# The opening of a four-layer fp32 kernel rebuilt around batch 0's chain, with idle transposes on TensorE

## Time and profile before

| | us |
|---|---|
| runs | 458.79, 456.85, 453.72 (median 456.85) |
| the profiled execution | 456.1, span 454.4, mean granted clock 0.966 |
| PE busy, PE weight loads busy | 395.8 (87%), 370.1 (81%) |
| DVE, ACT, POOL busy | 308.2 (68%), 226.6 (50%), 182.2 (40%) |
| PE in the chain that ended last | 50%; DVE 24%, ACT 12%, POOL 6% |
| `normalise(b, 0)` of the four batches starts at | 80.08, 175.77, 269.97, 364.14 |

### The profile page before, as it was taken

How to read it: one execution, slowest core, us unless ns; L and a number is a source line. 1 busy time by engine, 2 the same in 40 slices (tenths; PEclk the granted TensorE clock), 3 DMA queues, 4 the chain that set the end, 5 groups by cost and what they waited for, 6 DMA issues and landing times.

```text
span 454.4 us, 8501 instructions
## 1 busy us (share of the span) xinstructions
PE 395.8 (87%) x3034; PEld 370.1 (81%) x3034; DVE 308.2 (68%) x929; ACT 226.6 (50%) x622; POOL 182.2 (40%) x300
## 2 busy tenths in 40 slices
PE   0668747699998999999989999999899989998596
PEld 0546636599987998899979997999789979996495
DVE  3479767796786666878765758878665666765343
ACT  0285564456564344656644345656543456564132
POOL 2235283734553433455434334545533332322031
PEclk9988986899999999999999999999999999999699
DMA  7997001000000001100000002000000000000000
GB/s 212 364 343 282 1 0 50 1 2 1 1 0 3 0 1 30 45 1 1 2 1 1 1 1 72 2 1 2 1 1 2 1 23 1 2 2 0 0 1 23
DMA packets 15080, 16.85 MB, mean 37 GB/s; under 512 B 1536, under 2 KB 14016, under 8 KB 15040
## 3 DMA queue, kind: packets, MB, share of 16 engines
q1 hardware_dynamic: 15040, 16.33, 11.1%
HBM read 15.28 MB, written 1.05 MB: 36 GB/s over the span
## 4 chain that ended last, share of the span: by engine, by line
PE 50%; DVE 24%; ACT 12%; POOL 6%; issue 5%; DMA 2%; SPq 1%; DVEq 0%; POOLq 0%; ACTq 0%
PE bank_s L300 13%; PE bank_u L300 10%; PE bank_qa L300 6%; ACT prob L741 6%; DVE prob L1326 5%; PE bank_o L300 4%; PE bank_pt L300 4%; PE bank_pt L471 3%; DVE pt_lo L1337 3%; DVE xn L1140 2%; POOL prob L1000 2%; DVE ut_lo L1343 2%; DMA wq_raw<-in_wqT 2%; ACT ut_hi L707 2%; PE bank_s L568 2%
## 5 line engine op out<-in xcount | busy, mean ns | idle before, releaser
L1000 POOL TENSOR_SCALAR prob<-prob,row_inv,valid_b 128x256 f32<-128x256 f32 x128 | 71.5, 567 | 84.2 <-DVE row_inv L1333 83.6
L741 ACT ACTIVATE prob<-prob,row_min 128x256 f32<-128x256 f32 x128 | 64.1, 502 | 71.5 <-DVE row_min L1326 71.5
L1337 DVE TENSOR_TENSOR pt_lo<-bank_pt,pt_hi 128x512 fp32r<-128x512 f32 x64 | 44.2, 690 | 14.1 <-ACT pt_hi L707 13.8
L1343 DVE TENSOR_TENSOR ut_lo<-bank_u,ut_hi 128x256 fp32r<-128x256 f32 x64 | 27.0, 422 | 38.6 <-ACT ut_hi L707 38.2
L1326 DVE CUSTOM_DVE_ANT_0 prob<-bank_s,masked 128x256 f32<-128x256 f32 x128 | 48.9, 419 | 2.9 <-PE bank_s L300 2.3
L300 PE MATMUL bank_u<-pt_hi,cx_hi 128*128 128x256 f32 x128 | 37.8, 295 | 7.0 <-DVE pt_lo L1337 6.7
L1012 POOL TENSOR_TENSOR act_lo<-act_raw,act_hi 128x256 fp32r<-128x256 f32 x32 | 24.0, 749 | 48.0 <-ACT act_hi L800 48.0
L300 PE MATMUL bank_o<-c_hi,ut_hi 128*128 128x256 f32 x128 | 39.2, 306 | 4.5 <-DVE ut_lo L1343 4.5
L707 ACT ACTIVATE pt_hi<-bank_pt 128x512 fp32r<-128x512 f32 x64 | 37.5, 586 | 10.8 <-PE bank_pt L471 10.8
L471 PE MATMUL bank_pt<-ident,prob 128*128 128x128 f32 x256 | 39.4, 277 | 3.9 <-POOL prob L1000 3.6
L300 PE MATMUL bank_qa<-xt_hi,a_hi 128*128 128x256 f32 x128 | 41.0, 320 | 0.8 <-DVE qa_lo L1315 0.7
(11 more groups left out here) (234 smaller groups left out, 1300.7 us busy)
## 6 DMA issues: line engine op xcount, KB each, us to landing
wq_raw<-in_wqT SPq DMA_DIRECT2D x4, 512.0 KB, 8.8
wo_raw<-in_wo SPq DMA_DIRECT2D x4, 512.0 KB, 9.7
w_raw<-in_w12T SPq DMA_DIRECT2D x1, 1408.0 KB, 9.1
gate_raw<-in_gateT SPq DMA_DIRECT2D x2, 576.0 KB, 8.8
up_raw<-in_upT SPq DMA_DIRECT2D x2, 576.0 KB, 10.5
down_raw<-in_downT SPq DMA_DIRECT2D x2, 576.0 KB, 12.4
x<-in_x SPq DMA_DIRECT2D x4, 256.0 KB, 5.3
guT<-in_guT SPq DMA_DIRECT2D x4, 256.0 KB, 6.8
```

The source lines that it names most:

```text
L741: last = act.activation(row, row, ACT.Exp, scale=-1.0, bias=row_min[:, h % 2, t:t + 1], accum_out=row_sum[:, h % 2, t:t + 1])
L1000: last = pool.tensor_scalar(row, row, row_inv[:, h % 2, t:t + 1], valid_b[:, 0:1], ALU.mult, ALU.mult)
L1337: dve.tensor_tensor(pt_lo[:, :, :].rearrange("p s t -> p (s t)"), bank["pt"][:, :], f32(pt_hi[:, :, :].rearrange("p s t -> p (s t)")), ALU ...
L1343: dve.tensor_tensor(ut_lo[:, :], bank["u"][:, 0:T], f32(ut_hi[:, :]), ALU.subtract).then_inc(S["u_l"], 1)
```

## The change

- **Loads**: the ternary weights (w12 1408 KB, w3 704 KB) move ahead of Wk, Wq, Wv and Wo; the turned expert weights of one batch at a time are loaded, into one buffer, and the mask after.
- **Opening**: PE turns x of batch 0 only (and of batch 1 at its end); x of batches 2 and 3 is normalised, turned and measured in the FFN stage of the batch before the one ahead (`lnq_apply`, `q_weight_scales`, `q_first_scales` at c = 4, 6, 7; `q_turn_xn` on PE at c = 7). POOL's roots and first diagonals for them go between `ffn_low` and `normalise(b+1, 0)`.
- **TensorE**: 94 transposes of the unit matrix into the unused bank `pt`, in four calls of `keep_busy`.
- **Ternary weights** become (w > g) - (w < -g) with g = half the mean magnitude: POOL writes w < -g, DVE takes it from w > g; no ACT pass after. Layer 2's residual is scaled by 0.5 instead of w3.
- **Layer 1**: DVE writes batch 0's diagonals (128x128 each) instead of POOL; gate*up and silu go from POOL to DVE.
- **Prep banks**: 16 units use 6 banks instead of 2.
- **FFN weights**: 12 units of 128x576, all lo parts on POOL: 4 in the opening, 8 inside the heads of batch 0.

```diff
+        PREP_BANKS = ("qa", "o", "s0", "s1", "qa", "o", "s0", "s1", "qa", "o", "qa", "o", "x1", "pt", "o", "x1")
+FFN_LO_HEADS = (1, 2, 5, 6, 7, 8, 13, 14)
# SP
             turned_expert_weights(0)
             expert_weights(0)
+            ternary_weights()
             attention_weights(0)
+            mask(0)
# PE
+            def keep_busy(n):
+                for _ in range(n):
+                    pe.transpose(bank["pt"][:, 0:P], ident[:, :], ident[:, :])
             pe.wait_ge(S["consts"], 2)
-            q_turn_x0()
+            keep_busy(22)
+            q_turn_xn(0)
+            keep_busy(24)
+            q_piece(0, 0)
+            keep_busy(24)
             prep_unit(0)
-            q_piece(0, 0)
+            pe.wait_ge(S["abs_done"], 6)
+            pe.matmul(bank["u"][:, 0:6], ones[:, :], gsum[:, :], ...).then_inc(S["gamma_mm"], 1)
+            q_piece(1, 0)
             prep_unit(1)
+            q_piece(2, 0)
...
+            q_piece(5, 0)
+            q_piece(6, 0)
             prep_unit(7)
+            keep_busy(24)
+            bit_turn(0)
             prep_unit(8)
+            pe.wait_ge(S["limits"], 1)
+            pe.wait_ge(S["w12_ready"], 4)
+            pe.wait_ge(S["prep_lo"], 8)
# ACT
+            act.activation(warm[:, :], ones[:, 0:2], ACT.Exp)
+            act.wait_ge(S["w12_in"], 16)
+            for j in range(2):
+                for k in range(ND):
+                    magnitudes12(j, k)
+            act.wait_ge(S["w3_in"], 32)
+            magnitudes(...)  # w3, two parts
             prep_hi(0)
+            q_bf(0, 0)
# POOL
             q_round(0, 0, 0)
             q_scale_diagonals(0, 0)
+            pool.wait_ge(S["limits"], 1)
+            for j in range(2):
+                for k in range(ND):
+                    ternary12_minus(j, k)
+            q_root1(0)
+            ternary3_minus(0)
+            ternary3_minus(1)
             q_round(0, 1, 0)
             q_scale_diagonals(0, 1)
+            lnq_power(1, 2)
             power(0, "lnb")
+            pool.wait_ge(S["lnb_xn"], 1)
+            ffn_weights_lo(0)
             for c in range(BIT_CHUNKS):
                 bit_low(0, c)
             power(0, "lna")
+            pool.wait_ge(S["lna_xn"], 1)
+            ffn_weights_lo(1)
+            ffn_weights_lo(2)
+            ffn_weights_lo(3)
             normalise(0, 0)
+            q_roots(1)
+            q_spread_diagonals(1, 0)
# POOL, a head of a batch
                     if h == 13:
                         power(b + 1, "lnb")
+                    if b == 0 and h in FFN_LO_HEADS:
+                        ffn_weights_lo(FFN_LO_EARLY + FFN_LO_HEADS.index(h))
# POOL, the end of a batch
                 for c in range(FFN_CHUNKS - 1):
                     ffn_low(b, c)
+                if b + 2 < NB:
+                    q_roots(b + 2)
+                    q_spread_diagonals(b + 2, 0)
                 if not last:
                     normalise(b + 1, 0)
# DVE
             q_ctx_amax(0)
+            q_spread_diagonals0(0)
             q_scaled_w(0, 0)
...
             q_round_w0(0)
+            ternary_limits()
+            q_bf_w(0)
+            prep_lo(0)
             prep_lo(1)
             q_dequant(0, 0)
+            q_half_product(0)
+            q_silu(0)
+            ternary12(0, 0)
             q_ratio1(0)
+            ternary12(0, 1)
+            q_spread_diagonals0(1)
             prep_lo(2)
             q_scaled_w(0, 1)
...
             q_round_w0(1)
+            ternary12(1, 0)
             prep_lo(3)
+            lnq_stats_of([1]); lnq_variances([1])
             q_dequant(0, 1)
             q_residual0()
             ln_stats_of(0, "lnb")
             prep_lo(4)
             ln_apply(0, "lnb")
             prep_lo(5)
+            ternary12(1, 1)
             prep_lo(6)
             ln_lo(0, "lnb", xt_hi, xt_lo)
+            prep_lo(7)
+            ternary3(0)
+            ternary3(1)
# DVE, batch 0's head 9
+                    elif h == 9 and b == 0:
+                        link(lnq_stats_of([2, 3]))
+                        lnq_variances([2, 3])
```

More of the change, by code:

```diff
@@ L207, in build @@
                 S[f"{n}{i}"] = sem(f"{n}{i}_in")
-        for i in range(FFN_UNITS):
+        for i in range(FFN_LOADS):
             S[f"ffn_w{i}"] = sem(f"ffn_w{i}_in")
@@ L690, in _ @@
             queries(0, 1)
+            q_turn_xn(1)
+            prep_unit(14)
             pe.wait_ge(S["ctx_hi"], 1)
@@ L874, in _ @@
-            last.then_inc(S["next_xn"], 1)
-            prep_hi(6)
-            prep_hi(7)
+            for k in range(4, 7):
+                prep_hi(k)
             q_bf(0, 1)
             q_wscale(0, 1)
+            prep_hi(7)
+            for u in range(3):
+                ffn_weights_hi(u)
+            ln_hi(0, "lnb", xt_hi)
             prep_hi(8)
-            act.wait_ge(S["bit_q12"], 1)
-            for j in range(2):
-                act.activation(w12[:, :, j * BIT:(j + 1) * BIT], w12_raw[:, :, j * BIT:(j + 1) * BIT], ACT.Copy,
-                               bias=-MAGIC).then_inc(S["w12_ready"], 1)
-                if j == 0:
-                    prep_hi(9)
@@ L1442, in before @@
                 def before(h):
[L1443 to L1448 removed]
+                    if not last and h == 7:
+                        q_silu(nxt)
                 attention(b, before, beside)
@@ L1487, in batch @@
                             mask_row(nxt)
+                            if b + 2 < NB:
+                                lnq_apply(b + 2)
+                        if c == 6 and b + 2 < NB:
+                            q_weight_scales(b + 2)
                         if c == 5:
@@ L1530, in ternary @@
-            def ternary(part):
-                if part == 0:
-                    for j in range(2):
-                        w = w12_raw[:, :, j * BIT:(j + 1) * BIT]
-                        last = dve.tensor_scalar(w, w, gam[:, j:j + 1], MAGIC, ALU.mult, ALU.add)
-                    link(last)
-                else:
-                    dve.tensor_scalar(w12_raw[:, :, :], w12_raw[:, :, :], MAGIC + 1.0, MAGIC - 1.0, ALU.min, ALU.max
-                                      ).then_inc(S["bit_q12"], 1)
+                link(dve.tensor_scalar(gam[:, :], bank["u"][:, 0:6], 1.0 / (BIT * D), None, ALU.mult))
@@ new lines, in ternary_limits, with ternary12 @@
+                pairs = gam[:, :].rearrange("p (j k) -> p j k", k=2)
+                link(dve.tensor_tensor(above[:, :], pairs[:, :, 0], pairs[:, :, 1], ALU.add))
+                link(dve.tensor_scalar(above[:, :], above[:, :], BIT_EPS, 0.5, ALU.add, ALU.mult))
+                dve.tensor_scalar(below[:, :], above[:, :], -1.0, None, ALU.mult).then_inc(S["limits"], 1)
+            def ternary12(j, k):
+                dve.wait_ge(S["minus12"], 2 * j + k + 1)
+                cols = slice(j * BIT, (j + 1) * BIT)
+                dve.scalar_tensor_tensor(out=w12[:, k, cols], in0=w12_raw[:, k, cols], scalar=above[:, j:j + 1],
+                                         in1=f32(w12[:, k, cols]), op0=ALU.is_gt, op1=ALU.subtract
+                                         ).then_inc(S["w12_ready"], 1)
@@ new lines, in ternary3 @@
+            def ternary3(part):
+                dve.wait_ge(S["minus3"], part + 1)
+                rows, cols = ((P, slice(0, BIT_FULL)), (BIT_REST, slice(BIT_FULL, BIT_CHUNKS)))[part]
+                flat = [t[0:rows, cols, :].rearrange("p c d -> p (c d)") for t in (w3, w3_raw)]
+                dve.scalar_tensor_tensor(out=flat[0], in0=flat[1], scalar=above[0:rows, 2:3], in1=f32(flat[0]),
+                                         op0=ALU.is_gt, op1=ALU.subtract).then_inc(S["w3_ready"], 1)
```

495 lines of the change are left out of this document (224 added, 271 removed).

## The result

The changed kernel takes 459.26 us, the median of 20 runs (456.48 to 461.91); the kernel before takes 455.97 in 20 runs beside them. The ratio is 1.0082, with a 95% interval of 1.0063 to 1.01. The forecast of 447.0 and its range of 440 to 454 both miss. The profiled execution took 460.1, its span is 458.4 at a mean clock of 0.957; with 454.4 before, 4.0 us of span are to be explained, and 13.1 against the 445.3 forecast.

A forecast was written before the change was run, and what follows sets the result against it. It took the opening, up to about 80 us, as bound by a chain of hand-offs PE mostly waits for, later PE work. 454.4 − 11.5 + 2.4 gave 445.3 of span, plus 1.7: 447.0 us, range 440 to 454.

The forecast's parts named there:

- First scaling: First scaling on DVE in the opening: starts at 12.1 us instead of 17.10, 5.0 earlier.
- keep_busy: Four calls of added transposes on PE in the opening: they raise the clock and cost nothing.
- The rival by which transposes don't raise it: PE in the opening: transposes don't hold the clock; 7.7 us more, 454.7; chance 0.12.
- First rounded transposes: PE in the opening, waiting for Wq, taken as in at 17: 18.5 us instead of 21.45, 2.9 earlier.
- Second scaling: DVE in the opening, with POOL's 128x704 pieces at 1.2 us each: 31.2 instead of 33.96, 2.8 earlier.
- One wait of that step: DVE's gate*up, with two SBUF inputs, waits for POOL's last 128x704 piece: done at 24.6 us.
- Residual add: Residual add on DVE in the opening: at 37.4 us instead of 42.54, 5.1 earlier.
- layer 2's add: Layer 2's add on DVE, behind the ternary products: at 56.5 us, 4.9 earlier.
- Normalise of layer 2: DVE's normalise, for which POOL now waits: 0.73 us instead of 5.31, a further 4.6 earlier.
- From there on: From head 0's `pt_lo` to the end, heads and FFN stages: added work and savings sum to 2.4 us later.
- the lock costs little: DVE slips between POOL's pieces and neither hinders the other: 442.5 us; chance 0.18.
- the slower rival: POOL becomes late in every head of batch 0: 12.4 us more, 459.4; chance 0.07.

The follow-up runs named there:

- e1_pool_mult: The changed kernel with POOL's six comparisons (w < -g) written as multiplications, output not the reference's; median 453.16 us, ratio 0.9942.
- e1_again: The same kernel as e1_pool_mult run once more for a second profile; median 453.76 us, ratio 0.9965 to the kernel before.
- e3_no_busy: The changed kernel without its 94 transposes of the unit matrix; median 460.18 us, ratio 1.0107 to the kernel before.
- c2_more_busy: e2_dve_compare with 30 more transposes of the unit matrix on TensorE; median 452.52 us, ratio 0.9934 to the kernel before.
- d4_one_pass: c2_more_busy with one comparison (w > g) per ternary piece, output not the reference's; median 449.39 us, ratio 0.9868.
- e2_dve_compare: The changed kernel with the comparison w < -g moved from POOL to DVE, output the reference's; median 453.08 us, ratio 0.994.
- c1_junction: e2_dve_compare with POOL's root and diagonals for the batch after next placed behind `normalise(b+1, 0)`; median 452.14 us, ratio 0.99.
- d3_spread_first: The changed kernel with DVE comparisons, c3_banks' banks, added transposes, Wq loaded before ternary weights, second spread ahead of prep units 4 and 5; 453.3 us, ratio 0.9946.
- c3_banks: e2_dve_compare with prep units 6 and 7 in other banks and DVE's ternary pieces and lo parts reordered; median 451.68 us, ratio 0.9914.

## Why the prediction was wrong

Lengths between stations, in us. The last two columns have POOL's comparison replaced.

| stretch | forecast | after | e1_pool_mult | e1_again |
|---|---|---|---|---|
| start to rounded transposes | 18.5 | 19.05 | 17.17 | 19.88 |
| to second scaling | 12.7 | 19.00 | 12.27 | 12.73 |
| to layer 2's add | 25.3 | 28.76 | 28.43 | 28.46 |
| to `pt_lo` of head 0 | 16.8 | 18.62 | 17.29 | 17.41 |
| to the end of the span | 372.0 | 372.97 | 372.04 | 371.92 |
| span | 445.3 | 458.4 | 447.2 | 450.4 |

- *First scaling* and *keep_busy*: right (12.24 against 12.1; the calls cost nothing and hold the clock). The rival by which transposes don't raise it falls with e3_no_busy, and with it, for this kernel, the rule that the prediction cited from the Trainium skill (TensorE: Matmul & The Clock Gate, section Part 4: PE-mode transpose): the turn at 7.04, with only transposes ahead of it, took 0.66 us, and 1.09 without them.
- *First rounded transposes*: right for this profile (17.91 for Wq, 17 forecast). What I did not have is that Wq's arrival varies: unit 0 started at 16.03 to 18.29 in the twelve profiles of kernels that load it behind the ternary weights. The eleven of these kernels that have the transposes show what a late Wq does to the clock: with a wait of at most 2.8 us in front the unit took 1.16 us (five profiles), with 3.2 to 3.8 it took 1.16 or 1.17 in two and 2.07 or 2.08 in four. So a late Wq makes half speed likely, not certain.
- *Second scaling*: **the step that failed.** "Four pieces of 128x704 (1.2 each, by 1.96 for 1280)" took a comparison's price from a multiply-and-add. Each piece costs 2.64, the 1280 one 4.60. Of the 6.3 us in this stretch, 4.0 are the root, which waited until 31.27 behind the four pieces; 1.7 are the diagonals, done 4.7 us behind the root where I had 3.0, for the 1280 piece held them for its 4.60 (in my sum its 1.96 and the two diagonals' 0.54 make 2.5, not 3.0); and 0.6 is the spread, at half clock (1.22 us) after TensorE's idle time. The place of the root and of the diagonals was on record, the size was not. e1_pool_mult and e1_again give the 6.3 back in full.
- *One wait of that step never happened.* I had let DVE's gate*up wait for POOL's last 128x704 piece and be done at 24.6. It ran from 24.32 to 24.74, silu from 24.90 to 25.33, both with two SBUF inputs and both in the middle of POOL's second piece (22.72 to 25.35), at 0.43 each. That the ratio came on time in spite of the slow pieces (27.2, 26.7 forecast) is luck: had the exclusion held as I wrote it, all would have waited until 31.3.
- *Residual add* to *layer 2's add*: 3.5 too short. By stations it is 1.4 up to the residual add (7.56 us instead of 6.2), 0.3 up to the ternary products (7.90 instead of 7.6) and 1.8 in them (13.30 instead of 11.5). DVE's queue is a part of it (2.2 between c2_more_busy and d4_one_pass), the slow clock another (1.1 between e2_dve_compare and c2_more_busy); how they share the 3.5 in the changed kernel was not measured.
- *Normalise of layer 2*: right (0.74). The slow clock of 68 to 76 came back all the same: `pt_lo` is 1.8 later than forecast behind the add, and 0.5 in e1_pool_mult.
- *From there on*: 372.97 against 372.0, but in part by luck. It is 3.4 more than before where 2.4 had been forecast: 0.2 up to `normalise(0, 15)`, 1.5 from there to `normalise(3, 15)` (279.5 instead of 278.0; 1.1 of it in the two batches that have a junction, for which 1.8 had been counted), and 1.7 behind it, where the change does nothing. In that last part the clock was at its half level for about 10.2 us instead of 6.8, by the windows from 420 to 440. The FFN pieces cost 1.4 where 1.8 was counted. Which of the added pieces costs the 1.5 was not tested, save that POOL's roots and diagonals at the junctions don't (c1_junction).
- *The rivals*: "the lock costs little" is wrong for the long pieces (4.63 and 4.26), but right for POOL's 128x704 comparisons, beside which DVE's gate*up, silu and the ternary piece at 27.08 took their usual time. There the prediction's rule of an exclusion for a whole instruction did not hold. In the rival on the transposes, 25.4 is by its own terms where the turn ends (20.9, then 2.1, 0.4 and 2.0), but it was set against a start. In the slower rival the junctions go from 1.2 to 4.2, where the sum had 1.8. Its 459.4 meets the measured 459.26 by luck: POOL was late not in the heads but in the opening.
- *The level*: the opcode is about half of the miss. With it replaced the medians are 453.2 and 453.8, 5.5 to 6.1 below the changed kernel's and still 6 to 7 above the forecast, where the two profiled executions took 448.9 and 452.1. What those profiles show of the rest is Wq's arrival (rounded transposes at 17.17 and 19.88, 18.5 forecast), 3.1 to 3.2 before layer 2's add and 0.5 to 0.6 behind it. That the medians lie 1.6 to 4.2 above the two profiled executions stays unexplained beyond that. A kernel whose opening waits for a load of varying arrival should not be forecast from one profile. Without the failed step's cause the medians show a gain of 0.4 to 0.6% (453.2 to 453.8 against 455.5 to 455.7), not the 2% forecast.

So 94 transposes, a new load order and a rebuilt list earn about 10 us in the opening at best (`pt_lo` at 75.16 in e1_pool_mult, 84.80 before). In the changed kernel's profile one opcode on POOL and a Wq that came 1.9 us later take all of it back; in the median about 2 us of gain are left without the opcode.

## What to carry to other kernels

A duration belongs to an engine, a shape and an operation: before moving work to another engine with another opcode, find a row of that opcode there, or give it a range as wide as the lack of one. Look for what is queued behind the moved instruction and what runs beside it, since a long POOL instruction can be paid a second time by a DVE instruction that it locks out; but read from rows which pairs do exclude each other, for here one shape of the same POOL instruction did and another hardly did. When the chain is shortened, ask which engine's queue becomes the bound: here the residual add could be brought 3.7 us forward (d3_spread_first against c3_banks) and layer 2's add came 1.3 later.
